# Gated cross-attention and mixture of experts on one core: routing pieces in other gaps, and the experts' rows added as two chains of half rows

## What is computed

```
x = x + tanh(g0) * attention(layernorm(x), ctx, ctx)     # 16 heads of 64; the attention's output times q, then projected, plus bias
n = layernorm(x)                                         # 4096 rows
logits = n @ gate_w.T                                    # 8 experts
the two best of each row, weights = softmax of the two logits
x = x + tanh(g1) * sum over both experts: weight * (silu(n @ w1[e]) @ w2[e])   # F = 1024
```

## Time and profile before

| what | us |
|---|---|
| median of 3 runs (756.53 to 765.16) | 757.85 |
| the profiled execution | 760.15 |
| its span, first to last instruction | 758.4 |
| PE busy | 728.1 (96%) |
| DVE busy | 586.2 (77%) |
| POOL busy | 397.4 (52%) |
| ACT busy | 377.6 (50%) |

### The profile page before, as it was taken

How to read it: one execution, slowest core, us unless ns; L and a number is a source line. 1 busy time by engine, 2 the same in 40 slices (tenths; PEclk the granted TensorE clock), 3 DMA queues, 4 the chain that set the end, 5 groups by cost and what they waited for, 6 DMA issues and landing times.

```text
span 758.4 us, 23508 instructions
## 1 busy us (share of the span) xinstructions
PE 728.1 (96%) x7980; PEld 605.2 (80%) x7981; DVE 586.2 (77%) x1270; ACT 377.6 (50%) x671; POOL 397.4 (52%) x308
## 2 busy tenths in 40 slices
PE   7999999999999999998899999999999999999994
PEld 6567767767677766776899988999999999999993
DVE  5688879798897989796778778776767677777761
ACT  3686776767677667754344432333333333333331
POOL 5145445767576666674533648444444353444434
PEclk9999999999999999999999999999999999999998
DMA  8552353536282625433888885333333333333322
GB/s 293 161 145 108 140 167 116 180 128 225 77 286 78 231 98 182 153 116 93 254 224 223 228 205 123 53 52 50 49 49 49 50 47 54 49 51 49 51 37 29
DMA packets 93177, 93.88 MB, mean 124 GB/s; under 512 B 59312, under 2 KB 77936, under 8 KB 92720
## 3 DMA queue, kind: packets, MB, share of 16 engines
q1 hardware_dynamic: 31184, 64.97, 25.8%
q0 software_dynamic: 13392, 18.03, 13.7%
q10 hardware_dynamic: 48528, 9.92, 7.6%
HBM read 53.89 MB, written 37.95 MB: 121 GB/s over the span
## 4 chain that ended last, share of the span: by engine, by line
DMA 40%; issue 7%; POOL 3%; PE 1%; ACTq 1%; DVE 1%; ACT 1%; POOLq 0%; DVEq 0%
DMA out<-y,meta 40%; POOL records L1757 2%; POOL out L1751 1%; PE h_ps L1484 0%; ACTq L158 0%; ACT y L1556 0%; ACT hid L1549 0%; PE h_ps L1528 0%; DVE last_stats L1659 0%; DVE ht_l L1629 0%; POOLq L70 0%; ACTq L160 0%; DVE ht_h L1627 0%; ACTq L1535 0%; DVE bx L165 0%
## 5 line engine op out<-in xcount | busy, mean ns | idle before, releaser
L1751 POOL DMA_INDIRECT out<-y,meta x71 | 157.4, 2217 | 198.4 <-DMA out<-y,meta 178.8
L1484 PE MATMUL h_ps<-bx_h,w_now 128*128 128x128 f16 x2272 | 194.7, 219 | 3.0 <-DVE bx_l L1615 1.6
L1497 PE MATMUL pair_ps<-weights,ht_h 128*128 x1136 | 190.7, 273 | 1.9 <-issue 1.3
L1484 PEld LDWEIGHTS h_ps<-bx_h,w_now 128*128 128x128 f16 x2272 | 152.6, 98 | 6.8 <-DVE bx_l L1615 2.6
L1484 PE MATMUL h_ps<-bx_l,w_now 128*128 128x128 f16 x1136 | 156.4, 219 | 0.9 <-issue 0.9
L1497 PE MATMUL pair_ps<-weights,ht_l 128*128 x568 | 154.8, 273 | 0.0
L1497 PEld LDWEIGHTS pair_ps<-weights,ht_h 128*128 128x128 f16 x1136 | 110.2, 97 | 17.9 <-issue 3.4
L1556 ACT ACTIVATE y<-pair_ps,meta 128x256 f32<-128x256 f32 x71 | 33.7, 475 | 172.3 <-DVE meta L1610 114.8
L1306 POOL TENSOR_TENSOR r_l<-r,r_h 128x512 f16<-128x512 f32 x62 | 75.3, 1215 | 73.6 <-ACT r_h L832 71.7
L1627 DVE CAST ht_h<-hid 128x1024 f16<-128x1024 f32 x71 | 50.1, 706 | 81.5 <-ACT hid L1549 76.6
L1549 ACT ACTIVATE hid<-h_ps 128x1024 f32<-128x1024 f32 x71 | 72.7, 1023 | 62.7 <-PE h_ps L1484 59.6
(11 more groups left out here) (250 smaller groups left out, 1235.9 us busy)
## 6 DMA issues: line engine op xcount, KB each, us to landing
stage<-in_w SPq DMA_DIRECT2D x16, 1024.0 KB
w_split<-split SPq DMA_DIRECT2D x14, 1024.0 KB, 6.5
weights<-w_split SPq DMA_DIRECT2D x14, 1024.0 KB
rows<-records ACTq DMA_DIRECT2D x268, 32.0 KB
xin<-in_x SPq DMA_DIRECT2D x7, 512.0 KB, 5.4
x_even<-in_x SPq DMA_DIRECT2D x4, 512.0 KB
x_odd<-in_x SPq DMA_DIRECT2D x4, 512.0 KB
out<-x_even SPq DMA_DIRECT2D x4, 512.0 KB
```

The lines of the kernel that those rows point to most:

```text
L1484: last = nc.tensor.matmul(h_ps[r % 2][:, c, :], w1_now[:, r % 2, s, k * F + c * P:k * F + c * P + P], xt[:, r % 2, k, :], start=(j == 0 an ...
L1497: last = nc.tensor.matmul(y_ps[r % 2], ht[:, r % 2, c, :], weights_at(e, s, WN // 2 + c * D, D).rearrange("p o n -> p (o n)"), start=(c == ...
L1751: pool.indirect_dma_start(out, bass.IndirectOffsetOnAxis(meta[:, r, 0:1].bitcast(U32), 0), y[:, r % 2, :], None, compute_op=ALU.add).then_ ...
```

## The change

- `pick_rows` is split: `count_rows` (L250) goes to gap 1 of p = 5, the mask product stays in gap 3. `place_rows` goes from gap 1 of p = 5 to gap 4 of p = 4.
- A record has 259 values (ROW = D + 3): two row numbers, 2 * token and 2 * token + 1, and the weight. meta and meta_in have 3 columns. The counter of tokens goes up in twos.
- The output is seen as rows of 128 values. Each block is added by two indirect DMAs of 128 half rows, each half a chain on its own semaphore. weigh and copy_meta wait for both.
- In the experts' stage DVE's routing pieces go into the five gaps of steps 6, 7, 8 and 12, 13, 14. copy_meta(i) goes in front of split_h(i) of step i.
- HEAD is 24 instead of 20. The second layer norm's rstd of j = 1 on POOL runs one step later.
- At the end of the attention stage `rest_of_table` parts 4, 5, 6 run at p = 1, 2, 3 of the last pairs, behind `times_q`, which goes in front of `turn_rows`.
- The zeroing of the spare output rows is a plain DMA instead of an indirect one.

```diff
-ROW = D + 2
+ROW = D + 3
+def count_rows(nc, dve, job_ps, s, carry, g):
+    dve.wait_ge(s.route_ops, g * ROUTE + 5)
+    nc.vector.tensor_tensor(carry.next_row[:, :], job_ps[:, TG * E:(TG + 1) * E], carry.next_row[:, :], ALU.add).then_inc(s.pos_read, 1)
...
+    nc.vector.tensor_scalar(rec[:, :, :, D + 1].bitcast(U32), carry.tok_ids[:, :].unsqueeze(1).broadcast_to([P, 2, TG]), 1.0, None, ALU.add)
...
-            if p == 4 and gap == 1:
-                both_masks(nc, dve, route, routed, g - 2)
+            if p == 4:
+                if gap == 1:
+                    both_masks(nc, dve, route, routed, g - 2)
+                if gap == 4:
+                    place_rows(nc, dve, job_ps, route, routed, carry, g - 2)
             if p == 5:
                 if gap == 1:
-                    place_rows(nc, dve, job_ps, route, routed, carry, g - 2)
+                    count_rows(nc, dve, job_ps, routed, carry, g - 2)
...
+            if p < 5:
+                times_q(n - 5, NP + p - 5)
+            if p in (1, 2, 3):
+                rest_of_table(p + 3)
             if p == 2:
                 dve.wait_ge(carry.rows_in[0], BLOCK_LOADS)
                 turn_rows(nc, carry.xt, carry.rows, 0).then_inc(carry.x_turned, 1)
-            if p < 5:
-                times_q(n - 5, NP + p - 5)
...
-            if p == 3:
-                rest_of_table(4)
...
-                rest_of_table(5)
-        rest_of_table(6)
...
-    HEAD = 5 * RB
+    HEAD = 6 * RB
...
-            after(act, added, (i - 1) * 16)
-            nc.scalar.mul(y[:, r % 2, :], y_ps[r % 2], meta[:, r, 1:2]).then_inc(y_out, 1)
+            for half in range(2):
+                after(act, added[half], (i - 1) * 16)
+            nc.scalar.mul(y[:, r % 2, :], y_ps[r % 2], meta[:, r, 2:3]).then_inc(y_out, 1)
...
+            copy_meta(i, r)
             if isinstance(i, int) and i == 0:
-                copy_meta(0, 0)
...
             split_h(i, r)
             between(i, 3)
-            if there(i + 1):
-                copy_meta(i + 1, (r + 1) % RB)
             between(i, 4)
...
+            for j in range(2):
+                choose_at = 6 + j * BEHIND
+                if i == choose_at:
+                    if gap == 0:
+                        turn_logits(nc, dve, job_ps, route, routed, j)
+                    if gap == 1:
+                        best_logits(nc, dve, route, routed, j)
+                    if gap == 2:
+                        best_experts(nc, dve, route, routed, j)
+                    if gap == 3:
+                        choice_masks(nc, dve, route, routed, carry, j)
+                if i == choose_at + 1 and gap == 0:
+                    both_masks(nc, dve, route, routed, j)
+                if i == choose_at + 2:
+                    if gap == 0:
+                        place_rows(nc, dve, job_ps, route, routed, carry, j)
...
             pool.wait_ge(y_out, i + 1)
-            after(pool, added, i * 16)
-            pool.indirect_dma_start(out, bass.IndirectOffsetOnAxis(meta[:, r, 0:1].bitcast(U32), 0), y[:, r % 2, :], None,
-                                    compute_op=ALU.add).then_inc(added, 16)
+            for half in range(2):
+                after(pool, added[half], i * 16)
+                pool.indirect_dma_start(half_rows, bass.IndirectOffsetOnAxis(meta[:, r, half:half + 1].bitcast(U32), 0),
+                                        y[:, r % 2, half * D // 2:(half + 1) * D // 2], None,
+                                        compute_op=ALU.add).then_inc(added[half], 16)
```

More of the change, by code:

```diff
@@ L1156, in between @@
                 if gap == 3:
[L1157 removed]
+                    pick_rows(nc, dve, route, routed, g - 2)
                 if gap == 4:
@@ L1405, in experts @@
     loads = sem("weight_loads")
-    meta_done, w1_ready, h_mm, h_act, h_hi, h_lo, y_mm, y_out, added = (sem(n) for n in (
-        "meta_done", "w1_ready", "h_mm", "h_act", "h_hi", "h_lo", "y_mm", "y_out", "added"))
-    HEAD = 5 * RB
+    meta_done, w1_ready, h_mm, h_act, h_hi, h_lo, y_mm, y_out = (sem(n) for n in (
+        "meta_done", "w1_ready", "h_mm", "h_act", "h_hi", "h_lo", "y_mm", "y_out"))
+    added = [sem(f"added{half}") for half in range(2)]
+    HEAD = 6 * RB
     BEHIND = 6
@@ L1471, in _ @@
         sp.wait_ge(records_in, 2 * 2 * TG * 16)
-        sp.wait_ge(added, 16 * NB)
+        for half in range(2):
+            sp.wait_ge(added[half], 16 * NB)
     @block.tensor
@@ L1608, in copy_meta @@
             dve.wait_ge(rows_in[r], block_loads(i, r))
-            after(dve, added, (i - RB + 1) * 16)
+            for half in range(2):
+                after(dve, added[half], (i - RB + 1) * 16)
             nc.vector.tensor_copy(meta[:, r, :], meta_in[:, r, :]).then_inc(meta_done, 1)
@@ L1733, in between @@
         def between(i, gap):
-            if isinstance(i, int) and LATE_AT <= i < LATE_AT + 4:
+            if not isinstance(i, int):
+                return
+            for j in range(2):
[14 more added lines that the diff above has]
+                        place_rows(nc, dve, job_ps, route, routed, carry, j)
+                    if gap == 1:
+                        if j == 1:
+                            dve.wait_ge(carried_in, 16 * LEFT)
+                        record_weights(nc, dve, route, routed, carry, j, rec[j])
+                    if gap == 2:
+                        count_rows(nc, dve, job_ps, routed, carry, j)
+                        pick_rows(nc, dve, route, routed, j)
+                    if gap == 3:
+                        if j == 1:
+                            dve.wait_ge(routed.pos_read, 2)
+                            nc.vector.tensor_tensor(count1[:, :], carry.next_row[0:1, :], carry.region_start[:, :], ALU.subtract).then_inc(table_ops, 1)
+                            nc.vector.tensor_copy(pad_first[:, :], carry.next_row[0:1, :]).then_inc(pad_slots, 1)
+                        row_numbers(nc, dve, route, routed, carry, j, slot[j])
+            if LATE_AT <= i < LATE_AT + 4:
                 op = 2 + 5 * (i - LATE_AT) + gap
@@ L1746, in _ @@
     def _(pool):
+        half_rows = out.rearrange("n (s d) -> (n s) d", s=2)
         def step(i, r):
             pool.wait_ge(y_out, i + 1)
-            after(pool, added, i * 16)
-            pool.indirect_dma_start(out, bass.IndirectOffsetOnAxis(meta[:, r, 0:1].bitcast(U32), 0), y[:, r % 2, :], None,
-                                    compute_op=ALU.add).then_inc(added, 16)
+            for half in range(2):
+                after(pool, added[half], i * 16)
+                pool.indirect_dma_start(half_rows, bass.IndirectOffsetOnAxis(meta[:, r, half:half + 1].bitcast(U32), 0),
+                                        y[:, r % 2, half * D // 2:(half + 1) * D // 2], None,
+                                        compute_op=ALU.add).then_inc(added[half], 16)
         def scatter(records_of, slots_of, n, landed):
```

43 lines of the change are left out of this document (11 added, 32 removed).

## The result

The changed kernel took 767.77 us (median of 5 runs, 767.47 to 771.79) against 756.64 us (755.73 to 765.16) of the kernel before, ratio 1.0111, 95% interval 1.0072 to 1.0150: slower by 1.1%. The forecast was 749.8 with a range of 744 to 757.5. The profiled execution took 771.79 us, its span is 770.1 us, 11.7 longer than before. The granted clock is 0.990 over the span.

The account below looks back on a forecast made before the run. PE was taken to bound the steady stretch, with the add chain trailing. Terms -4.4 - 0.8 + 0.5 - 3.5 = -8.2 us against the median 757.85 gave 749.6, said as 749.8; range 744 to 757.5.

Parts of the forecast that it names:

- A: Attention stage, routing: reading the counters in gap 1 ends PE's wait for next_row; -4.4 us, bounds -5.4 and -0.5.
- B: Change from attention to experts' stage: DVE's table parts done earlier let the new stage start sooner; -0.8 us.
- Rival 3: Attention stage: the routing gain moves to later PE waits for xt_lo or ssub; -1 us there, total 753.1; chance 0.12.
- C, the adds: Experts' first 25 blocks: two half adds at 1.75 us each bring POOL to 7.8 us in blocks with two scatters.
- 9.6 us of lag a job: Experts' scatter blocks: POOL's lag, 4 x 2.4 us; y's double buffer forgives about 5, some 4 us left.
- The term +0.5: Experts' first 25 blocks, all effects together: +0.5 us, bounds -4 and +10.
- C, the load: Experts' blocks while weights load, to about 450 us: half chains hide each other's landing, so lag before the scatters is smaller.
- rival 4: Scatter blocks: POOL becomes the bound if a half add's mean exceeds about 2.2 us; +11 there, total 760; chance 0.14.
- C, copy_meta: Experts' first 25 blocks: copy_meta before split_h finds its wait for adds already met; gain 0 to 3 us.
- The gaps and HEAD 24: Experts' stage: routing pieces spread over five gaps gain 0 to 1 us; HEAD 24 unrolls one trip more, same steps.
- D: Steady stretch and tail: half adds catch up with y; steady stretch gains nothing, tail shortens; -3.5 us.
- Rival 2: Steady stretch and tail: half chains lock to w_now's copy like the whole one; tail only -0.7, total 752.5; chance 0.12.

## Why the prediction was wrong

- **A and B** were right: 4.75 us for 5.2, and no new wait of size on PE in the attention stage. Alone they hold to the end (0.9935; 4.4 + 0.8 of 757.85 is 0.7%). Rival 3 is out.
- **C, the adds,** is the step that failed. Its numbers of POOL were good: "now 5.77 + 2.05 = 7.8" was 8.1 and 8.0, and the half add's mean was 1.85 us over the kernel and 2.06 from 415 to 500 us, for 1.75. What failed is what was made of the 9.6 us of lag a job: "of which y's double buffer ... forgives about 5", so "some 4 us a job". From the first half add of block 7 (415.85) to that of block 17 (490.76) POOL took 74.9 us for ten blocks, 21.7 more than PE's 53.2. From y's start to its add it was 3.0 us at block 7, 8.2 at block 11, 2.8 at block 13 and 8.5 at block 17. So 5.5 were forgiven over the ten blocks, not 5 in each job, and 16.2 were paid, where the kernel before pays 5.0 over the same ten blocks (y of block 7 at 410.49 to that of block 17 at 468.73). Between the jobs the lag did fall, but not because POOL caught up: it made 5.2 us a block there, no faster than PE. The y's came later, and PE with them. Nor was the buffer free to begin with: the kernel before ran 5.6 to 7.3 us behind in blocks 9 to 16 by the same measure, with whole adds. The term +0.5 measured +19.4 in the profiles; 17.6 of it goes with the half rows (137.9 us with whole rows), the rest is within what one profile can tell.
- **C, the load.** That the two half chains hide each other's landing, for which rival 4 counts 2 us, did not show. Up to block 6 the changed kernel was 4 us ahead. First half adds then went at 394.15, 400.53, 408.08 and 415.85, rounds of 6.4, 7.6 and 7.8 us; the kernel before made 5.7, 6.8 and 6.1 in the same blocks. The rstd and the last group's records came late behind them. Blocks 7 to 9 lost 8 us, and the lower clock cost more in block 10. In time this part is small: half rows up to block 6 alone cost 0.2%.
- **C, copy_meta** was forecast at "gain 0 to 3" and cost some 0.5%, 4 us. I asked whom the copy waits for, which was right (DVE's copy never waits for an add any more), and not who waits for the copy. The gaps and HEAD 24 at nothing were right.
- **D** had the right mechanism, and a size that this pair of profiles puts at -2.2 for -3.5, the means over all profiles at -3.2. From h1 to the end are 3.81 us, forecast 3.85; y to h0 was forecast at 0.6 and is 2.03, because h0(70) waits 1.30 us for the landing of h0(69). That wait differs from profile to profile: the same round, h0(69) to h0(70), is 764.44 - 759.74 = 4.70 us here and 3.93 to 4.95 in the seven other kernels that end in half rows. Rival 2, the lock to the copy, did not come: w_now's copy runs from 605.62 to 606.81, and the half adds issued at 606.46 and 608.53 take 1.77 and 1.55 us.
- **The rivals.** Rival 4 was the right mechanism, at a chance of 0.14. Its price (C +11, measured +19.4) was too small, and the point from which it decides, a mean half add of 2.2 us, was too high: the mean was 2.06 and it came all the same. An estimate by the sum above: 26 x (t + 0.3) + 28 = 69 gives t = 1.3 us, and with the 75.6 us that the kernel before really took for these blocks 1.5; both are less than the undisturbed 1.55. That sum over the stretch could have been made from the earlier trace rows. I made it block by block and forgave the rest.

## What to carry over

Where a change gives an engine more work in a stretch, as here two adds a block to POOL, add up its work over the whole stretch against the pace of the bounding engine, and only then ask what a buffer forgives; it forgives once, and only what is not yet in use. A wait counts by whether it reaches the bounding engine: ACT waited longer for adds with whole rows (75.0 us) than in the changed kernel (68.2), and nothing was lost by it. Splitting an indirect DMA by columns halves its bytes and not its rows, and here the issuing engine paid twice. When a step that releases a buffer is moved, list who waits for it, not only what it waits for.

## What was new about the hardware

- A half row of 512 bytes costs POOL the same as one of 1 KB: 1.55 us undisturbed for 128 rows in both kernels.
- Half the bytes don't shorten a chain's round reliably: at the end of the kernel, from the first half add of block 69 to that of block 70, it is 3.9 to 5.0 us in the eight kernels with two half chains there, and 4.3 to 4.6 in the twelve with one whole chain.
- After PE had stood idle for 5.2 us up to 418.02, the next 4 us ran at a granted clock of 0.50, so that a stall of 5 us cost 2 more in the block behind it. Not every stop does this: from 480 to 485 us PE was busy for 2.14 of 5 us, and the granted clock stayed at 1.00.
